# A two-layer graph network in 32-bit: the gated sum in two one-pass parts, the inverse root on GpSimd

## What is computed

```python
h = x @ W_loop.T
g = h @ Wg_loop.T
vals = (h + b_loop) * sigmoid(g + bg_loop)
x1 = layernorm(x + relu(adj.T @ vals))          # eps 1e-5, no scale or shift
y = (adj @ x1) @ weight[0] + bias
out = layernorm(x1 + y)
```

## Time and profile before

| | |
|---|---|
| time, median of 3 runs | 164.57 us (163.58 to 165.59) |
| span of the profiled execution | 162.0 us |
| PE busy | 150.9 us (93%) |
| PE weight loads busy | 139.8 us (86%) |
| DVE busy | 146.8 us (91%) |
| ACT busy | 126.8 us (78%) |
| POOL busy | 78.8 us (49%) |
| moved by DMA | 42.76 MB |

### The profile page before, as it was taken

The page is one execution under the profiler, slowest core; times in us unless marked ns, Lnnn a source line. Parts: engine busy times, 40 slices in busy tenths (PEclk is TensorE's granted clock), DMA queues, the critical chain, the costliest instruction groups (busy, mean ns, idle before and its releaser), DMA issues.

```text
span 162.0 us, 3905 instructions
## 1 busy us (share of the span) xinstructions
PE 150.9 (93%) x1064; PEld 139.8 (86%) x1064; DVE 146.8 (91%) x585; ACT 126.8 (78%) x287; POOL 78.8 (49%) x193
## 2 busy tenths in 40 slices
PE   7989999999999999999999999999999999999800
PEld 3668899999999999999999999999999999999700
DVE  1289999999999999999999999999999999999980
ACT  3376567699998888998888888888998887798260
POOL 2903571747556463636474745646363544422040
PEclk9999999999999999999999999999999999999975
DMA  4999999996999979697989899897979260011135
GB/s 133 274 386 402 398 398 396 396 384 222 295 337 272 355 222 391 177 379 227 350 263 334 294 286 360 234 384 209 366 212 345 51 225 35 35 66 65 65 128 210
DMA packets 19322, 42.76 MB, mean 264 GB/s; under 512 B 2145, under 2 KB 2785, under 8 KB 19297
## 3 DMA queue, kind: packets, MB, share of 16 engines
q1 hardware_dynamic: 14112, 25.24, 43.9%
q0 software_dynamic: 4752, 16.78, 32.9%
q10 hardware_dynamic: 432, 0.46, 0.8%
HBM read 34.08 MB, written 8.39 MB: 262 GB/s over the span
## 4 chain that ended last, share of the span: by engine, by line
issue 38%; POOL 33%; DVE 17%; DMA 6%; ACT 1%; POOLq 1%; PE 1%; DVEq 0%; ACTq 0%
POOL x L344 22%; DMA adj_sb<-adj_dram 4%; POOL adj_sb L322 4%; POOL adjt_sb L329 4%; POOL nmr L338 3%; DVE s_sb L805 2%; DVE last_stats L840 2%; DVE stats L812 2%; DMA w_all<-w_loop_dram 1%; DVE stats L827 1%; DVE z_sb L852 1%; POOLq L57 1%; DVE tiny L735 1%; DVE z_sb L823 1%; ACT out_sb L597 1%
## 5 line engine op out<-in xcount | busy, mean ns | idle before, releaser
L409 PE MATMUL hg_ps<-w_all,xt_sb 128*128 128x256 f32 x256 | 60.5, 380 | 0.0
L344 POOL TENSOR_SCALAR x<-s_sb,rstd,nmr 128x128 f32<-128x128 f32 x120 | 52.3, 445 | 3.3
L409 PEld LDWEIGHTS hg_ps<-w_all,xt_sb 128*128 128x128 f32 x256 | 46.6, 192 | 5.4 <-issue 0.3
L563 ACT ACTIVATE hg_ps<-gate_b 128x1024 f32<-128x1024 f32 (+1 forms) x32 | 32.0, 1002 | 7.2 <-DVE vals L797 6.6
L338 POOL TENSOR_TENSOR nmr<-mean_neg,rstd 128x4 f32<-128x4 f32 x31 | 6.2, 198 | 63.8 <-DVE rstd L758 63.8
L597 ACT ACTIVATE out_sb<-z_sb,rstd 128x128 f32<-128x128 f32 x108 | 36.7, 391 | 0.5 <-DVE rstd L758 0.5
L424 PEld LDWEIGHTS loop_ps<-vals,adj_sb 128*128 128x128 f32 x256 | 33.2, 191 | 3.4 <-DMA adj_sb<-adj_dram 1.1
L424 PE MATMUL loop_ps<-vals,adj_sb 128*128 128x128 f32 x256 | 34.0, 276 | 0.9 <-DMA adj_sb<-adj_dram 0.7
L445 PE MATMUL msg_ps<-adjt_sb,x 128*128 128x128 f32 x248 | 32.9, 276 | 0.2
L572 ACT ACTIVATE gate<-hg_ps 128x512 f32<-128x512 f32 x32 | 19.0, 595 | 15.4 <-PE hg_ps L409 15.3
L445 PEld LDWEIGHTS msg_ps<-adjt_sb,x 128*128 128x128 f32 x248 | 30.2, 192 | 0.5 <-issue 0.5
(11 more groups left out here) (77 smaller groups left out, 113.0 us busy)
## 6 DMA issues: line engine op xcount, KB each, us to landing
xt_sb<-x_t_dram SPq DMA_DIRECT2D x32, 256.0 KB, 6.5
x_sb<-x_dram SPq DMA_DIRECT2D x32, 256.0 KB, 6.7
adjt_sb<-adj_t_dram POOLq DMA_DIRECT2D x16, 512.0 KB, 6.8
out<-out_sb SPq DMA_DIRECT2D x31, 256.0 KB, 4.0
adj_sb<-adj_dram POOLq DMA_DIRECT2D x15, 512.0 KB, 4.6
adj_sb<-adj_dram POOLq DMA_DIRECT2D x2, 256.0 KB, 7.2
out<-out_sb ACTq DMA_DIRECT2D x1, 256.0 KB, 3.5
const_sb<-consts_dram SPq DMA_DIRECT2D x1, 192.0 KB, 5.9
```

Source lines behind the costliest of these rows:

```text
L344: done = nc.gpsimd.tensor_scalar(x1[:, q % X1_RING, batch(b)], s_sb[:, q % S_RING, batch(b)], r[:, b:b + 1], n[:, b:b + 1], ALU.mult, ALU.add)
L409: last = nc.tensor.matmul(hg_ps[:, q % 2, b, :], xt_sb[:, q % XT_RING, batch(b)], w_gate, start=False, stop=True, skip_group_check=True)
L563: nc.scalar.activation(hg_ps[:, q % 2, 0:graphs, :], gate_b[:, None, :].broadcast_to([P, graphs, 2 * P]), ACT.Copy).then_inc(seeded, 1)
```

## The change

- **Loop sum.** values still writes vals in 32-bit. DVE then rounds it into parts[0] (type float32r, rounded, line 732 of the new code), POOL subtracts this from vals into parts[1] (L314), and loop_sum runs two matmuls for each graph, one per part, both accumulated in the same place. The adjacency is declared float32r.
- **Inverse root.** The nine DVE operations go. DVE writes var (and mean_neg), POOL raises it to the power -0.5 for both norms in one operation on 128 x 8 (L320). norm1 subtracts the mean and multiplies in one operation, so that nmr goes too, but for the last two groups.
- **Order and lags.** Message weights and second sum come at lag 3 (before 4 and 5), the second root at 4 and norm2 at 5 (before 6 and 7). On PE the messages stand between two halves of project. On ACT a seed comes one step ahead of its use and ahead of the copy, norm2 is in one piece, and look reads two groups at once, every second step. SP stores one step after norm2.
- **Drain.** Only the last two groups are special. The last norm2 is shared by DVE and ACT, the one of group 29 is POOL's; each of the last three second roots is a power of its own.

```diff
-LOOP_LAG, NORM1_LAG, MSG_LAG, Y_LAG, Z_LAG, STAT2_LAG, NORM2_LAG = 1, 2, 3, 4, 5, 6, 7
+LOOP_LAG, MSG_LAG, Y_LAG, Z_LAG, NORM2_LAG = 1, 3, 3, 3, 5
+ROOT1_LAG, ROOT2_LAG = 1, 4
...
+            def rest(q):
+                pool.wait_ge(hi_done, q + 1)
+                nc.gpsimd.tensor_tensor(parts[:, q % 2, 1, :], vals[:, q % 2, :], parts[:, q % 2, 0, :].bitcast(F32),
+                                        ALU.subtract).then_inc(lo_done, 1)
+
+            def roots(c, first, end):
+                pool.wait_ge(var_done, c)
+                await_count(pool, out_done, c - RSTD_RING - ROOT2_LAG + 1)
+                nc.gpsimd.tensor_tensor(rstd[:, c % RSTD_RING, first:end, :].rearrange("p l b -> p (l b)"),
+                                        var[:, c % 2, first:end, :].rearrange("p l b -> p (l b)"),
+                                        power[:, first:end, :].rearrange("p l b -> p (l b)"), ALU.pow)\
+                    .then_inc(root_done, 1)
...
-            for t in range(GROUPS + NORM1_LAG - 1):
-                norm1(t - NORM1_LAG)
+            for t in range(GROUPS):
+                rest(t)
+                if t >= 1:
+                    roots(t, 0, 2)
+                    norm1(t - 1)
                 if t % 2 == 1:
                     load_adj(t // 2 + 3)
                     load_adjt(t // 2 + 2)
...
-                    pe.wait_ge(vals_done, q + 1)
+                    pe.wait_ge(lo_done, q + 1)
 
                     await_count(pe, s_done, q)
                     for b in range(GB):
-                        last = nc.tensor.matmul(loop_ps[:, batch(b)], adj_sb[:, spot, batch(b)],
-                                                vals[:, q % 2, batch(b)], start=True, stop=True)
+                        for part in range(2):
+                            last = nc.tensor.matmul(loop_ps[:, batch(b)], adj_sb[:, spot, batch(b)],
+                                                    parts[:, q % 2, part, batch(b)], start=part == 0, stop=part == 1)
                     last.then_inc(loop_done, 1)
...
             for t in range(GROUPS):
-                project(t)
+                project(t, (0, 1))
+                messages(t - MSG_LAG)
+                project(t, (2, 3))
...
                 loop_sum(t - LOOP_LAG)
                 message_weights(t - Y_LAG)
-                messages(t - MSG_LAG)
+            messages(GROUPS - 3)
             loop_sum(GROUPS - 1)
-            inject(GROUPS - 4)
-            messages(GROUPS - 3)
-            message_weights(GROUPS - 4)
-            inject(GROUPS - 3)
+            message_weights(GROUPS - 3)
             messages(GROUPS - 2)
-            message_weights(GROUPS - 3)
+            message_weights(GROUPS - 2)
             messages(GROUPS - 1)
-            message_weights(GROUPS - 2)
+            inject(GROUPS - 1)
+            message_weights(GROUPS - 1)
...
             for t in range(GROUPS):
-                copy_messages(t - Y_LAG)
-                norm2(t - NORM2_LAG, (0, 1))
+                seed(t + 1)
+                if t % 2 == 0:
+                    look(t // 2 - 1)
+                copy_messages(t - MSG_LAG)
                 gates(t)
-                norm2(t - NORM2_LAG, (2, 3))
-                look(t - 1)
-                seed(t + 2)
+                norm2(t - NORM2_LAG, every)
...
+            def variances(c, first, end):
+
+                for q, done in ((c - ROOT1_LAG, bn1_done), (c - ROOT2_LAG, bn2_done)):
+                    await_count(dve, done, min(q, GROUPS - 1) + 1)
+                await_count(dve, root_done, c - 2)
+                both = stats[:, c % STATS_RING, 2 * first:2 * end, :].rearrange("p c (i k) -> p (c i) k", k=3)
+                if first == 0:
+                    await_count(dve, x1_done, c - 2)
+                    ts(mean_neg[:, c % 2, :], both[:, 0:GB, 1], -1.0, None, ALU.mult)
+                ts(var[:, c % 2, first:end, :].rearrange("p l b -> p (l b)"), both[:, :, 2], 1.0 / P, EPS,
+                   ALU.mult, ALU.add).then_inc(var_done, 1)
...
+            def rounded(q):
+                dve.wait_ge(vals_done, q + 1)
+
+                await_count(dve, loop_done, q - 1)
+                nc.vector.tensor_copy(parts[:, q % 2, 0, :], vals[:, q % 2, :]).then_inc(hi_done, 1)
...
             for t in range(GROUPS):
...
+                values(t)
+                if t == 0:
+                    message_weight()
+                if exists(t - LOOP_LAG):
+                    first_sum(t - LOOP_LAG)
+                rounded(t)
+                if exists(t - LOOP_LAG):
+                    first_stats(t - LOOP_LAG)
+                    variances(t, 0, 2)
+                if t == 2:
+                    message_weight_end()
                 if exists(t - Z_LAG):
                     second_sum(t - Z_LAG)
...
+                    second_stats(t - Z_LAG)
```

More of the change, by code:

```diff
@@ new lines, in norm1 @@
+            def norm1(q):
+                c = q + ROOT1_LAG
+                pool.wait_ge(root_done, c)
+                await_count(pool, msg_done, q - X1_RING + 1)
+                await_count(pool, z_done, q - X1_RING + 1)
+                for b in range(2 if q in SHARED else GB):
+                    done = nc.gpsimd.tensor_scalar(
+                        x1[:, q % X1_RING, batch(b)], s_sb[:, q % S_RING, batch(b)],
+                        mean_neg[:, c % 2, b:b + 1], rstd[:, c % RSTD_RING, 0, b:b + 1], ALU.add, ALU.mult)
+                done.then_inc(x1_done, 1)
@@ L402, in _, with project @@
             pe.wait_ge(seeded_dve, 1)
-            def project(q):
+            def project(q, graphs):
                 if exists(q):
@@ L407, in project @@
                     pe.wait_ge(seeded, q + 1)
-                    for b in range(GB):
+                    for b in graphs:
                         last = nc.tensor.matmul(hg_ps[:, q % 2, b, :], xt_sb[:, q % XT_RING, batch(b)], w_gate,
                                                 start=False, stop=True, skip_group_check=True)
-                    last.then_inc(hg_done, 1)
+                    if graphs[-1] == GB - 1:
+                        last.then_inc(hg_done, 1)
             def loop_sum(q):
@@ L553, in _ @@
             nc.scalar.activation(table[:, :], half[:, :], ACT.Sigmoid)
+            every = tuple(range(GB))
             def seed(q):
@@ L657, in copy_turned @@
+            norm2(GROUPS - 2, every)
+            norm2(LAST, (2, 3))
             def copy_turned(step, ways):
@@ L882, in find_odd @@
-            def find_odd():
-                dve.wait_ge(seen_done, GROUPS)
-                nc.vector.tensor_reduce(worst[:, :], seen_sum[:, :], AX_X, ALU.max).then_inc(odd_ready, 1)
-                yield
-                dve.wait_ge(odd_ready, 1)
-                ts(odd[:, :], worst[:, :], W / 4 + 0.5, None, ALU.is_gt).then_inc(odd_ready, 1)
-            for t in range(GROUPS):
-                steps = chain(t)
-                def step(n):
-                    for _ in range(n):
-                        next(steps, None)
+                await_count(dve, out_done, q - Z_RING + 1)
@@ new lines, in second_sum, with second_stats @@
+                tt(z_sb[:, q % Z_RING, :], y_of(q, 0), x1[:, q % X1_RING, :], ALU.add).then_inc(z_done, 1)
+            def second_stats(q):
+                if q == LAST:
+                    dve.wait_ge(y_done, q + 1)
+                else:
+                    dve.wait_ge(z_done, q + 1)
+                for p in range(2):
+                    z = y_of(q, 2 * p) if q == LAST else z_sb[:, q % Z_RING, :]
+                    got = nc.vector.bn_stats(
+                        stats[:, (q + ROOT2_LAG) % STATS_RING, 2 + p, :],
+                        z[:, 2 * p * P:2 * (p + 1) * P].rearrange("p (i n) -> p n i", i=2))
+                got.then_inc(bn2_done, 1)
@@ L916, in _ @@
-                step(CHAIN_OPS)
-                if t == 2:
-                    message_weight_end()
-            steps, last_steps, odd_steps = chain(LAST_CHAIN - 1), chain(LAST_CHAIN), find_odd()
-            next(steps)
-            next(steps)
-            next(steps)
-            first_sum(GROUPS - 1)
-            next(steps)
-            first_stats(GROUPS - 1, 0)
-            next(steps)
-            first_stats(GROUPS - 1, 1)
-            next(steps)
-            for _ in steps:
-                next(last_steps)
```

402 lines of the change are left out of this document (121 added, 281 removed).

## The result

The changed kernel takes **202.25 us** (median of 4 runs, 200.99 to 203.77) beside 164.12 for the kernel before in the same session: a ratio of 1.2325, 95% interval 1.2264 to 1.2387. I had forecast 159.5 us and a range that ended at 172. It was wrong in sign and by 42.75 us.

A forecast was written before the change was run, and what follows sets the result against it. PE and DVE were taken as both full, with POOL fullest after the change. Project 5 at 25.65 + 26 steps of 4.25 + drain 16.5 + 6.82 = 159.5 us, in short 49.0 + 26 steps; range 153 to 172.

The forecast's parts named there:

- The bound: POOL becomes the fullest engine at 4.16 us a step, beside PE 4.03, DVE 4.06 and ACT 3.8.
- The power: POOL's inverse root on 128x8, put at 0.40 us between bounds of 0.20 and 1.8.
- my 4.25: Forecast step in us: the longest engine, POOL at 4.16, plus 0.09 for engines waiting on each other.
- the rival that won, at 0.13: POOL's unknown prices: a power of 1.0 us makes the step 4.85 and the time 175 us; chance 0.13.
- norm1: Four norm1 operations on POOL take 1.74 us in a step, as before the change.
- The subtraction and the copy: Subtraction on POOL 1.2 us, upper bound 2.1; rounding copy on DVE 0.40, between 0.29 and 0.60.
- The new record: PE's loop sum group of eight one-pass matmuls takes 0.52 us, between bounds of 0.44 and 1.78.
- the rival at 0.11: The new record is no shorter: loop sum stays 0.89 us, PE 4.40 a step, 163.8 us; chance 0.11.
- The port: Rival: DVE's var waits 0.45 us each step for POOL's subtraction, step about 4.6, 168.6 us; chance 0.14.
- Fill: Start of the run: loop sum 0 at 12.5, 2.2 us later; project 5 at 25.65 instead of 22.85.
- Drain: From project 31 to the end of the last norm2: 16.5 us, 3.5 less than before.
- the third sign: The forecast is wrong if PE has no gaps and loop sums of 0.89 us.

The follow-up runs named there:

- e1: The changed kernel with GpSimd's power replaced by a multiplication, so the inverse root is left out: 168.08 us (ratio 1.0251).
- e3: The changed kernel with the loop sum as one 32-bit matmul per graph again, no rounding copy or subtraction, power kept: 165.81 us (ratio 1.0128).
- e2: As e1, but mean_neg and var made by DVE reductions, scale and epsilon left out: 165.72 us (ratio 1.0104).
- e4: As e1, but the loop sum has four matmuls of 256 columns instead of eight of 128, values wrong: 167.05 us.
- e5: As e1, but the loop sum's eight matmuls are cut to 64 columns each, half of the products left out: 167.83 us.

## Why the prediction was wrong, point by point

**The bound, right.** I said POOL goes from the emptiest to the fullest engine, and that subtraction and power together may take 1.8 us before the gain is gone. They take 1.27 + 1.65 = 2.92.

**The power, the step that failed.** "I take 0.40, near the row with the same kind of instruction." The bounds were 0.20 and 1.8; the value is 1.65, almost the upper one, which is luck: that bound was nine tiny steps, and the power is one instruction. The tiny product that I leaned on has the same form, and e1 shows it: as a product this very instruction takes 0.20. The operation, not the form, sets the price: 1.65 us for 8 elements and 1.01 for 4, so 0.16 for an element and 0.37 beside. The sum of POOL with what it measured is 1.27 + 1.65 + 1.94 + 0.58 = 5.44 us, with 0.11 between the instructions 5.55, the step. Of the 1.30 us over my 4.25 the power is 1.25. "If the power takes 1.0 us ... 175 us" was the rival that won, at 0.13; with 1.65 its own formula gives a step of 4.16 + 1.25 + 0.09 = 5.5, and 49.0 + 26 x 5.5 = 192.

**norm1, mis-sized.** I carried 1.74 over; it takes 1.89 to 1.98 in the middle of the run, 1.94 in the mean. Its instructions (least, median, most in ns), after and then in e3:

```profile
L332 POOL TENSOR_SCALAR x<-s_sb,mean_neg,rstd x124: 441/447/736, 18.5 to 188.7; 128x128 f32<-128x128 f32 x124
```

```profile
L327 POOL TENSOR_SCALAR x<-s_sb,mean_neg,rstd x124: 448/452/454, 15.1 to 152.1; 128x128 f32<-128x128 f32 x124
```

Most last as before and 30 last over 500 ns; with the copy and the subtraction gone none does. The copy on DVE (0.42 us, SBUF to SBUF) is what the long ones meet: all 30 overlap it in the trace, and of the 72 that don't none lasts over 464 ns. In e1, which has the copy too, one norm1 meets it, and that one alone is long (693 ns). So the copy holds norm1 up as the subtraction holds mean_neg up; a run without the copy alone was not made.

**The subtraction and the copy, right.** 1.27 for my 1.2, 0.42 in the median and 0.47 in the mean for my 0.40. The Trainium skill (GPSIMD Engine Reference, section 3.1), from which I worked out an estimate of 1.1 to 1.2 us, agrees within 0.2.

**The new record, wrong.** "I take 0.52, near the lower bound"; it is 0.91, the rival at 0.11. The sentence that failed is "so time goes with columns": it was read from records of 256 and 128 columns of the 32-bit type (0.216 and 0.111), and in the new type 64 columns take 0.112 as 128 do, and 256 take 0.119., which I cited for that rival, had it: 256 loads for 256 records, as busy as the records. In the changed kernel this cost nothing, since POOL was the bound; but it means that the split has no gain on PE to pay with. Its best case, e2 with no port wait and no root, has PE full at 4.40 us, as before.

**The port, right in mechanism, wrong in chance and place.** I had var waiting 0.45 us for 0.14 of the chance; mean_neg, which stands ahead of it, waits 0.8 in the mean (0.985 - 0.17), and 1.9 where POOL issues transfers ahead of the subtraction. In e3, with no subtraction on POOL, it lasts 0.17 in the median and 0.28 at most. What I held against it, a minimum of 152 ns, was no measure of it, since L735 met POOL's short norm1 where mean_neg meets a subtraction of 1.27. The rule of the Trainium skill (SBUF — State Buffer, section Who interferes with whom) agrees with the rows in that the wait ends with POOL's instruction; the 2.04 us differ in that they run past the end of two issues to the end of the subtraction behind. The 0.16 of L746 beside an issued transfer shows that not all of POOL's work does it. By that rule alone I had 168.6, and e1, which has the port's wait without the power, gave 168.08; that these are so near is partly luck, since e1's step is 4.47 and not 4.6, and its project 5 comes at 27.84, 2.2 us later than I had it. The record, longer than that sum had it, is hidden there: with shorter ones in e4 the time is still 167.05.

**Fill.** Loop sum 0 at 12.5 was right (12.21). Project 5 at 25.65 was not (30.52): three powers of 1.65 stand ahead of it on POOL, and the steps of 5 to 6 us begin there. And PE, idle for 3.05 us ahead of loop sum 0, came back at half speed: the granted clock is 0.67 and 0.64 in the stretches from 10 to 20 us, between its two levels of 1.2 and 2.4 GHz, the first loop sum lasts 1.94 us for 1.16, and project 2 lasts 3.72 for 1.89. I had named this as 1 to 2 us; these two alone are 2.6, partly hidden, since PE waits 0.53 us for norm1 right behind.

**Drain.** I had 16.5 and it took 20.4. From loop sum 31 on I had 0.69 + 6.9 + 2.3 = 9.9, and e1 with its cheap product takes 10.47, so the plan of the drain was about right; with powers it takes 12.56, as two of 1.65, the first in part, and one of 1.0 stand on the path. The other 1.3 us lie ahead of loop sum 31: 7.9 us from project 31 for my 7.3 - 0.69, at POOL's pace.

**What I said would show it wrong** came: mean_neg over 0.5, power over 0.8. Of the third sign, half: loop sums of 0.91, but with gaps on PE (17.15 of 20 us busy).

## What to carry to other kernels

An operation that the trace does not show is priced by the operation and not by the shape of a row that looks like it: when its bounds are a factor of nine apart and it lands on an engine with no room, work out the time at both bounds and let the range hold both (here 1.8 would have given 196). When two parts of a change go to the same engine, work out each alone and both together; here each alone cost 5 to 7 us and the two 41. And before a matmul is cut into cheaper passes, see whether its weight loads are as long as its records: here, where they were, fewer columns brought nothing, and fewer records, each with its load, were what made the group shorter.

## What the runs showed of the hardware that I had not expected

- The power on POOL takes 1.65 us for 128x8 and 1.01 for 128x4, the product of the same form 0.20.
- Records with 128 stationary columns start 0.112 us apart with 64 moving columns, 0.112 with 128 and 0.119 with 256, in the one-pass type (inside a group; e5, e1 and e4).
- Tiny DVE operations with all operands in SBUF lasted up to 2.3 us beside POOL, both as one-source (mean_neg, 2.04) and as two-source (var, 2.32), in part while POOL only issued transfers; reductions of the same tiles lasted 0.15 to 0.16 always.
- A norm1 operation on POOL that met DVE's copy lasted up to 0.74 us, for 0.45 without it.
